# Sixteen-batch hybrid block on one core: new places for every stage in the engines' programs, with places of their own for batch 0 and batches 11 to 15

## The reference

```python
x = x + mamba(layernorm(x))      # a: RMS norm, conv of 4 taps, scan over 16 states, out and feed-forward
x = x + experts(layernorm(x))    # e1
x = x + ssm(layernorm(x))        # b: gates, a scan over 16 states, tanh, out
x = x + experts(layernorm(x))    # e2, the same weights as e1
```

```python
def step(h, t):                  # mamba, per channel d and state n
    h = jnp.exp(d_t[:, :, None] * A) * h + (d_t * u_t)[:, :, None] * B_t[:, None, :]
    return h, jnp.einsum('bdn,bn->bd', h, C_t)
def experts(x):                  # 8 heads, the best of 32 x 32 keys, one expert each out of 8192
    index, score = best_pair(x @ w_q, keys)
    h = gelu(einsum('bnd,bnhd->bnh', x, w_down[index])) * relu(score)
    return einsum('bnh,bnhd->bnd', h, w_up[index])
```

## Time and profile before

| | us |
|---|---|
| median of three runs | 2152.82 (2145.71 to 2153.90) |
| the profiled execution, its own time | 2153.84 |
| span in its trace | 2152.1 |
| DVE, PE, ACT, POOL busy in the span | 1724.8, 1668.6, 1547.5, 1356.2 |
| end of the gate (L1435) of batches 8, 9, 14, 15 | 1152.2, 1273.5, 1748.7, 1874.1 |

### The profile page before, as it was taken

How to read it: one execution, slowest core, us unless ns; L and a number is a source line. 1 busy time by engine, 2 the same in 40 slices (tenths; PEclk the granted TensorE clock), 3 DMA queues, 4 the chain that set the end, 5 groups by cost and what they waited for, 6 DMA issues and landing times. The chain is left out here.

```text
span 2152.1 us, 23261 instructions
## 1 busy us (share of the span) xinstructions
PE 1668.6 (78%) x6097; PEld 925.3 (43%) x6186; DVE 1724.8 (80%) x4157; ACT 1547.5 (72%) x3340; POOL 1356.2 (63%) x1209
## 2 busy tenths in 40 slices
PE   4887878787888988887878879787878886755563
PEld 2333435354444445454544445454534443443342
DVE  3888989798988989898988899898989897733331
ACT  4566767587878978787878779787978775555443
POOL 0225454577676777677776767677677777566554
PEclk8899998999998999998999999998999898877766
DMA  2001111122222232222322222222323222233222
GB/s 55 0 10 50 39 57 33 52 74 81 77 76 80 76 87 71 82 74 66 93 79 77 76 73 77 84 72 70 84 77 83 79 76 79 71 87 94 79 81 71
DMA packets 79876, 150.76 MB, mean 70 GB/s; under 512 B 20584, under 2 KB 46592, under 8 KB 79680
## 3 DMA queue, kind: packets, MB, share of 16 engines
q0 software_dynamic: 49152, 134.28, 22.0%
q1 hardware_dynamic: 29344, 14.65, 2.4%
q10 hardware_dynamic: 1248, 0.34, 0.1%
HBM read 145.01 MB, written 4.19 MB: 69 GB/s over the span
## 5 line engine op out<-in xcount | busy, mean ns | idle before, releaser
L1453 POOL DMA_INDIRECT rows<-in_experts,index x1024 | 981.1, 958 | 461.6 <-issue 370.2
L1347 DVE TENSOR_TENSOR_SCAN hp<-dA,fed_ps 128x1024 f32<-128x1024 f32 x256 | 582.3, 2275 | 3.4 <-DVE fed_ps L1331 0.5
L773 PE MATMUL ysum<-hp,ident 128*128 128x512 f32 x1024 | 496.3, 629 | 16.5 <-DVE hp L1357 11.8
L1468 POOL TENSOR_TENSOR hp<-hp,c_row 128x1024 f32<-128x1024 f32 x112 | 263.9, 2356 | 254.0 <-ACT c_row L1037 152.2
L1331 DVE TENSOR_TENSOR fed_ps<-du,b_ps 128x1024 f32<-128x1024 f32 x256 | 312.7, 1222 | 45.7 <-PE b_ps L748 27.6
L1020 ACT ACTIVATE dA<-delta,decay 128x511 f32<-128x511 f32 x512 | 334.5, 710 | 11.5 <-issue 6.8
L999 ACT ACTIVATE rows<-rows,coef 128x128 f32<-128x128 f32 x1024 | 310.9, 390 | 22.1 <-DVE coef L1268 21.9
L1261 DVE CUSTOM_DVE_ANT_0 rows<-rows,xn 128x128 f32<-128x128 f32 x1024 | 268.1, 324 | 62.6 <-DMA rows<-in_experts,index 62.3
L773 PEld LDWEIGHTS ysum<-hp,ident 128*128 128x128 f32 x1024 | 211.0, 207 | 246.1 <-issue 209.0
L923 ACT ACT_TABLE_LOAD x218 | 279.7, 1283 | 8.8 <-PEq L533 4.9
L706 PE MATMUL bank<-rows,ident 128*128 128x256 f32 x1024 | 249.6, 400 | 32.7 <-ACT rows L999 31.1
(11 more groups left out here) (183 smaller groups left out, 2323.7 us busy)
## 6 DMA issues: line engine op xcount, KB each, us to landing
rows<-in_experts,index POOLq DMA_INDIRECT x1024
x_in<-in_x SPq DMA_DIRECT2D x16, 256.0 KB
x_res<-in_x SPq DMA_DIRECT2D x16, 256.0 KB
y<-x SPq DMA_DIRECT2D x16, 256.0 KB
rows<-in_taps SPq DMA_DIRECT2D x1, 512.0 KB
rows<-in_wq_t SPq DMA_DIRECT2D x1, 512.0 KB, 4.9
rows<-in_in_proj_t ACTq DMA_DIRECT2D x1, 256.0 KB
rows<-in_key_t SPq DMA_DIRECT2D x1, 128.0 KB, 5.1
```

The source lines that it names most:

```text
L773: mm = nc.tensor.matmul(ysum[:, j, :], ident[:], hp[:, BUFFER[k], j, :], start=(k == SUM_ORDER[0]), stop=(k == SUM_ORDER[-1]))
L1347: nc.vector.tensor_tensor_scan(flat, dA[:, n % NDA, :, :].rearrange("p a b -> p (a b)"), fed_ps[:].rearrange("p a b -> p (a b)"), 0.0, ALU ...
L1453: pool.indirect_dma_start(e.rows[:, t, h, :], None, A["experts"], bass.IndirectOffsetOnAxis(ap=e.index[:, t, h:h + 1], axis=0)).then_inc(e ...
L1468: pool.tensor_tensor(state, state, c_row[:, k % NCR, :].unsqueeze(1).to_broadcast([P, NH, T]), ALU.mult).then_inc(pool_read, 1)
```

## The change

No operation and no buffer is added or taken away. SLOTS has new numbers, most of them one to five slots away from the old; LAST_SLOTS and FIRST_SLOTS are gone, and a table BATCH_SLOTS gives places to single batches: 0 (the start), 11, 12, 13, 14 and 15 (the end). A batch's own place now holds in whichever iteration it falls; before, the end's places held from iteration 15 on. `due` is rewritten for that. Line numbers of the change are those of before plus 197.

```diff
-    "pe_sim_e1": (POST, (35, 38, 44, 46)),
+    "pe_sim_e1": (POST, (34, 38, 44, 46)),
...
-    "dve_dot_e1": (POST, (53, 59, 75, 80)),
+    "dve_dot_e1": (POST, (52, 63, 74, 76)),
...
-    "dve_dot_e2": (POST, (214, 224, 228, 236)),
+    "dve_dot_e2": (POST, (220, 224, 229, 236)),
...
-    "pool_x3": (POST, (136,)),
-    "pool_fetch_e1": (POST, (43, 43, 47, 47, 61, 61, 61, 62)),
+    "pool_x3": (POST, (121,)),
+    "pool_fetch_e1": (POST, (38, 40, 44, 44, 59, 61, 63, 64)),
...
-LAST_SLOTS = {
...
+BATCH_SLOTS = {
+    0: {
+        "pe_skip": (59,),
...
 def due(stage, i, q, slot):
...
-    phase, slots = SLOTS[stage]
...
-    last = i >= LATE and stage in LAST_SLOTS
...
+    phase, own = SLOTS[stage]
+    for m in range(NB):
+        for k, place in enumerate(BATCH_SLOTS.get(m, {}).get(stage, own)):
+            if (m - OFFSET[phase] + place // TURN, place % TURN) == (i, slot):
+                yield m, m % 2, k
```

More of the change, by code:

```diff
@@ L63 @@
     "pe_out": (POST, (0,)),
-    "pe_ff1": (POST, (1,)),
-    "pe_ff2": (POST, (6,)),
+    "pe_ff1": (POST, (2,)),
+    "pe_ff2": (POST, (7,)),
     "pe_ln_a": (POST, (8,)),
     "pe_turn_e1": (POST, (31,)),
-    "pe_sim_e1": (POST, (35, 38, 44, 46)),
-    "pe_flip_e1": (POST, (41, 48)),
-    "pe_code_e1": (POST, (42, 50)),
-    "pe_sum_e1": (POST, (89, 98)),
+    "pe_sim_e1": (POST, (34, 38, 44, 46)),
+    "pe_flip_e1": (POST, (40, 49)),
+    "pe_code_e1": (POST, (43, 49)),
+    "pe_sum_e1": (POST, (89, 97)),
     "pe_turn_b": (POST, (117,)),
[L73 to L81, removed]
+    "pe_xp": (POST, (120,)),
+    "pe_gate": (POST, (123,)),
+    "pe_y": (POST, (127,)),
+    "pe_z": (POST, (142,)),
+    "pe_ln_c": (POST, (146,)),
+    "pe_turn_e2": (POST, (175,)),
+    "pe_sim_e2": (POST, (176, 179, 184, 185)),
+    "pe_flip_e2": (POST, (181, 189)),
+    "pe_code_e2": (POST, (181, 197)),
     "pe_sum_e2": (POST, (237, 251)),
@@ L95 @@
     "act_gelu": (POST, (3,)),
[L96 to L98 removed]
+    "act_rstd_a": (POST, (4,)),
+    "act_rstd_e1": (POST, (22,)),
+    "act_norm_e1": (POST, (26,)),
     "act_turn_e1": (POST, (30,)),
[L100 removed]
+    "act_flip_e1": (POST, (42, 47)),
     "act_gelu_e1": (POST, (65, 83)),
[L102 to L103 removed]
+    "act_scale_e1": (POST, (71, 72, 84, 89)),
+    "act_out_e1": (POST, (92, 97)),
     "act_rstd_b": (POST, (103,)),
[L105 to L106 removed]
+    "act_norm_b": (POST, (109,)),
+    "act_turn_b": (POST, (121,)),
     "act_xp": (POST, (124,)),
[L108 removed]
+    "act_gate": (POST, (126,)),
     "act_tanh": (POST, (129,)),
[L110 removed]
+    "act_rstd_c": (POST, (141,)),
     "act_rstd_e2": (POST, (162,)),
[L112 removed]
+    "act_norm_e2": (POST, (172,)),
     "act_turn_e2": (POST, (174,)),
@@ L115 @@
     "act_gelu_e2": (POST, (223, 236)),
[L116 removed]
+    "act_scale_e2": (POST, (227, 234, 243, 243)),
     "act_out_e2": (POST, (237, 255)),
@@ L142 @@
-    "sp_xres": (POST, (33,)),
+    "dve_dot_e1": (POST, (52, 63, 74, 76)),
+    "dve_weigh_e1": (POST, (70, 83)),
+    "dve_stats_b": (POST, (100,)),
+    "dve_shift_b": (POST, (106,)),
+    "dve_scan_b": (POST, (126,)),
+    "dve_x3": (POST, (152,)),
+    "dve_stats_e2": (POST, (161,)),
+    "dve_shift_e2": (POST, (172,)),
+    "dve_top_e2": (POST, (178, 180, 183, 184)),
+    "dve_index_e2": (POST, (181, 198)),
+    "dve_dot_e2": (POST, (220, 224, 229, 236)),
+    "dve_weigh_e2": (POST, (225, 243)),
@@ L228, in summed @@
     return SUM_ORDER.index(n)
-def offset(phase, slot):
-    return OFFSET[phase] - slot // TURN
 def due(stage, i, q, slot):
-    phase, slots = SLOTS[stage]
-    if i == -1 and stage in FIRST_SLOTS:
-        slots = FIRST_SLOTS[stage][1]
-    last = i >= LATE and stage in LAST_SLOTS
-    for k, own in enumerate(slots):
-        new = LAST_SLOTS[stage][1][k] if last else own
-        both = last and i == LATE and new // TURN < own // TURN
-        for x in (own, new) if both else (new,):
-            o = offset(phase, x)
-            assert -DEPTH <= o <= OFFSET[phase] and new // TURN <= own // TURN
-            if x % TURN == slot and 0 <= i + o < NB:
-                yield i + o, (q + o) % 2, k
+    phase, own = SLOTS[stage]
[3 more added lines that the diff above has]
+                yield m, m % 2, k
 def at(b, per, k=0):
```

368 lines of the change are left out of this document (284 added, 84 removed).

## The result

| | before | the change |
|---|---|---|
| median, us | 2153.36 (2145.71 to 2155.64, 4 runs) | 2192.93 (2173.89 to 2201.77, 4 runs) |
| ratio | | 1.0178 [1.0106, 1.0250] |
| the profiled execution, us | 2153.84 | 2191.49 |
| its span, us | 2152.1 | 2189.7 |
| end of the last gate, us | 1874.1 | 1872.9 |

The change is slower by 1.8%, with an interval from 1.1% to 2.5%. The forecast was 2143.0 us, the range ended at 2176. In the two profiled executions the whole difference lies behind the last gate: up to there the changed kernel is 1.2 us ahead, and the tail is 38.8 us longer.

The account below looks back on a forecast made before the run. DVE was taken to bound middle iterations, POOL's nearly unbroken fetches the tail. Profiled 2153.84 + 1 (start) - 3 (iterations 0 to 3) - 27.5 (iterations 4 to 14) + 18.7 (tail) = 2143.0 us; range 2102 to 2176.

Parts of the forecast that it names:

- Batch 13 to 14: Tail, POOL's gap between these batches' e2 fetches: 15.9 us in place of 6.3, +9.6 (0 to +11).
- Part 4 of batch 15's e2: Tail: this part also waits for index_e2.1, which stands behind the dot of the tile before; +8.0 us (0 to +9).
- Batch 14 to 15: Tail, POOL's gap between these batches' e2 fetches: 11.0 us in place of 7.3, +3.7 (0 to +6).
- PE's sum now comes behind `code`: Tail, gap between the e2 fetches of batches 14 and 15: step in the chain forecast at 11.0 us.
- the 1.9 us for gelu: Tail, gap between the e2 fetches of batches 14 and 15: ACT's gelu ahead of flip, counted at 1.9 us.
- The start of batch 15's e1: Tail: index about 4 us later lets this fetch start at 1928.6 rather than 1931.21; -2.6 us (-11 to 0).
- The middle: Iterations 4 to 14: -2.5 us each (-5 to +1.5), times 11 -27.5; iterations 0 to 3 another -3.
- the terms for `offx` and for scan 13: Middle iteration: x3 leaving the place behind x1, -1.2 us; the dot going first behind scan 13, -1.1 us.
- The 3.39 us before `top_e1.3` stay: Middle iteration: DVE's wait for PE there is unchanged, as sum and sim keep their slots; 0 (-3.4 to +1).
- the other moves: Middle iteration: norm stages, weigh and norm_b on ACT, moved on engines with 20 us of room; 0.
- The slower one: Rival: the tail pays +18.7 us and the middle's gain is waited away before top_e1.3; 2173.5 us, chance 0.22.
- The stall moves: Rival: two POOL instructions in a row hold code as before, middle iterations gain only 1.2 us; 2158.8 us, chance 0.14.

Follow-up runs that it names:

- e4: The change with the order of before put back at three places of the tail; 2154.31 us, ratio to before 1.0059.
- e7: e4 with the last part of batch 14's e1 fetch moved earlier (slot 67 to 58); 2148.18 us, ratio to before 1.0031.
- e10: e9 with batch 15's sim and top moved ahead of PE's sum_e1.1; 2161.41 us, ratio to before 1.0014.
- e1: The change's places for the middle, with the old start and old end of the kernel before; 2129.46 us, ratio to before 0.9944.
- e2: The kernel before's middle places, with the change's own places for batches 12 to 15 and part of batch 11; 2196.71 us, ratio to before 1.0250.
- e5: The kernel before with dot_e1.0 alone moved right behind the scan of state 13 (slot 53 to 52); 2136.73 us, ratio to before 0.9976.
- e6: The kernel before with POOL's x3 alone moved behind the readout of state 13 (slot 136 to 121); 2142.93 us, ratio to before 1.0013.
- e9: e7 with weigh_e1.1 of batch 14 moved earlier, right behind dot_e1.3; 2165.66 us, one execution, no ratio.
- e12: e10 with POOL's x1 of batch 15 moved ahead of two parts of batch 12's e2; 2153.03 us, ratio to before 1.0054.

## Why the prediction was wrong

The profiled execution is 48.5 us over the forecast. Of these, 20.1 us lie in the tail, 15.8 in iterations 13 to 15 (forecast 5 us shorter, measured 10.8 longer), 12.3 in iterations 1 to 12 (25.5 shorter forecast, 13.2 measured) and 0.2 in the start.

**The bound and the mechanism of the tail were right, its price was not.** The tail was forecast at 297 us and took 316.8.

- *Batch 13 to 14* was forecast at 15.9 us of idle time and has 16.46. The links that the prediction named are in the timeline of the changed kernel, DVE first:

```profile
2035.54 0.29 DVE L1458 CUSTOM_DVE_ANT_0 rows<-rows,xn 128x128 f32<-128x128 f32 x1 [9.75 <-DMA rows<-in_experts,index]
...
2037.24 0.69 DVE L1425 TENSOR_REDUCE top<-bank 128x16 f32<-128x512 f32 x1
...
2048.82 0.19 DVE L1441 TENSOR_SCALAR bits<-bank 128x32 int32<-128x32 int32 x1 [10.00 <-PE bank L889]
```

```profile
2039.80 4.85 PE L903 MATMUL bank<-rows,ident 128*128 128x256 f32 x16
...
2046.63 0.61 PE L877 MATMUL bank<-ident,mask 128*128 128x128 bf16 x8
```

`top` stands behind the dot, the sum behind `top`, `flip` behind the sum. e4 gave the 9.8 us back by undoing it.

- *Part 4 of batch 15's e2* was forecast at a wait of about 10 us and has 9.63. e4 gave it back.
- *Batch 14 to 15* was forecast at 11.0 us and has 18.37. The step that failed is "PE's sum now comes behind `code`", from which only a saving was drawn. A fetch's parts 0 and 4 wait not only for the index, but also until PE has summed the batch before, whose rows lie in the same buffer (`e.summed` in `fetch`, two lines that stand directly behind the excerpt shown ahead of the prediction, which counted three waits). The chain that ended last shows it: `index` was ready at 2107.4, the sum at 2116.7.

```profile
2102.82 2.43 ACT rows L1196 x8
2105.26 1.03 ACT flip L1173
...
2107.25 0.19 DVE index L1450
...
2107.48 2.09 PE bank L866 x2
...
2112.35 4.33 PE bank L903 x16
```

Up to the index, the forecast's own chain took 2107.4 + 0.8 - 2099.1 = 9.1 us, where it said 11.0: the 1.9 us for gelu were 0.1. The rest is a sim, a top with its mask, and the sum.

- *The start of batch 15's e1* was forecast to come 2.6 us earlier, and comes 7.3 us later. POOL is free 10 us earlier, as forecast (1920.9 against 1930.9). But the index came at 1936.5 and not at about 1928: the prediction followed one wait, for the last part of batch 14's e1. e7 took that wait away and the gap was 10.3 us, against 11.2 in e4. Of the 7.3 us, 4.1 are gone in e4, which runs the same program up to there with a higher granted clock (0.92 and not 0.52 around the sum); the forecast had no term for that. The other 3.2 are gone in e10, after three moves, but one execution each does not show which of them, or whether the clock, brought it. **This stays open.**

**The middle has the right sign and less than half the size.** Forecast: -2.5 us an iteration, -30.5 us with iterations 0 to 3. e1, which has the new middle alone, is 12 us faster than before (7 to 17). The nine profiles with the new middle have 117.5 us a middle iteration on the average, before and e2 118.8: -1.3; with e5 and e6 the old middle has 118.2, -0.7. The lengthening fell by more than the terms for `offx` and for scan 13 said (4.4 us measured, not 2.3), because the dots and `offx` no longer meet readouts at several places. The step that failed is "The 3.39 us before `top_e1.3` stay" and the 0 for "the other moves": the waits did not stay where they were. Less idle time stands ahead of `top` (84.1 us in the whole span for 133.5), and more ahead of `bits`, for PE's `code` (80.6 for 46.9), and ahead of both indexes. On the profiled run this gave nothing, since iterations 13 to 15 lost what 1 to 12 won: the twelve are 13.2 us shorter, the three 10.8 us longer, and the start 1.2 us later. The prediction gave iterations 13 and 14 a gain of 2.5 each and 15 nothing: that is a second step that failed, since the own places of batches 11 to 15 act there too. With them, these three iterations took 368 us on the average of six profiles with the new middle, without them 359 of four; e2, with the old middle, took 372.0, before 360.6. In all seven profiles with the new end DVE is idle for 2.2 us ahead of the last gate, in those with the old end for 0.5 to 0.8. What the rest of the 9 us is stays open.

**The rivals.** The slower one had the mechanism (price in the tail, the middle's gain waited away, released by PE), with a chance of 0.22 and a price of 18.7 that was half of what it cost; its 2173.5 us is what the fastest of the four runs took (2173.89), which is luck. "The stall moves" is seen in e6, where x3 alone wins nothing. The Trainium skill (SBUF — State Buffer, section "SBUF: two separate sides") has the loser of the port wait for the whole instruction. `score` and `index` of the changed kernel end 0.03 us behind the readout of state 1 and x1, and the rows agree so far. It prices single meetings, and no run here shows a kernel whose time follows their sum: 4.4 us of lengthening less an iteration made it 0.7 to 1.3 us shorter.

The forecast of -27.5 for the middle and +18.7 for the tail were of one size, so that each error of the size of one of its terms decided the sign.

## What to carry to other kernels

When work is moved ahead of a fetch's index, list every semaphore that the fetch's first part waits for, the buffer's reuse among them, and follow each back; the one that was never late before may be the last one now. Time that an engine wins by shorter instructions should be priced only up to its next wait for another engine, here a sixth to a third of it. At the end of a pipeline, where one queue runs without a break, an order in which an instruction of the next batch stands behind the last tile of this one costs the whole chain behind it, once per batch. And a gap is a loss only against a fixed event: an engine that is free 9 us earlier and waits 9 us more has lost nothing.

## What had not been expected of the hardware

TensorE's granted clock differs just behind the last gate. Windows of the kernel before (columns as in the earlier trace rows):

```profile
1834.00:1874.00 40.00, 34.17 (x120) 18.05 (x120) 32.03 (x80) 22.55 (x53) 23.26 (x21) 0.88 0.25 71
1874.00:1884.00 10.00, 7.40 (x41) 4.45 (x40) 3.96 (x31) 4.95 (x6) 8.30 (x9) 1.00 0.30 88
```

Of the changed kernel:

```profile
1833.00:1873.00 40.00, 29.28 (x101) 16.55 (x101) 27.68 (x77) 18.00 (x38) 24.11 (x25) 0.87 0.28 79
1873.00:1883.00 10.00, 8.81 (x24) 4.15 (x24) 1.86 (x2) 4.24 (x11) 6.14 (x6) 0.66 0.28 79
```

Before, PE had 2.4 GHz in the first 10 us of the tail (1.00); in the changed kernel it had the lower level, 1.2 GHz, in two thirds of them (0.66), after 40 us in which it was busy 29.28 us and not 34.17. Four matmuls of `out` took 1.98 us before (L846) and 3.78 after (L1043):

```profile
1876.38 1.98 PE L846 MATMUL bank<-ucs,w_out 128*128 128x512 f32 x4 [0.86 <-ACT xnbT L1064]
```

```profile
1877.77 3.78 PE L1043 MATMUL bank<-ucs,w_out 128*128 128x512 f32 x4
```

This goes with the order: in all seven profiles with the new end (the change, e2, e4, e7, e9, e10, e12) these 10 us stand at 0.66, after 40 us with PE busy 29.3 to 29.5 us; in the seven with the old end at 0.96 to 1.00, after 33.0 to 34.8. It does not by itself make batch 15's e1 late, since e10 has the 0.66 too. Where the two levels fall after that differs between executions of one program, as the change and e4 showed. Over the change's four runs the time goes roughly with the mean clock of the run: 2173.89 us at 0.895, 2191.49 at 0.886, 2194.36 at 0.887, 2201.77 at 0.882. Which of the two sets the other is not shown.
